# GpSimd makes half of a quantised product, and ScalarE weighs half of the last chunk's experts by token

## The chip, the cores and the metric

The kernel runs on one core of a Trainium2 chip. The core's engines each work through an instruction stream of their own and wait for each other by semaphores: TensorE (PE), VectorE (DVE), ScalarE (ACT), GpSimd (POOL), and SyncE (SP), which issues DMAs. The metric is the device time of one execution in microseconds, median of several.

## What is computed

Two layers, each a chain of four parts on 2,048 tokens of 128 features. The change touches two of them. The third part of layer 0 is a gated network with fake quantisation: activations to 16 bits with one scale for the whole tensor, so each scale needs the maximum over everything.

```python
def act_qdq(x):
    qmax = 2.0 ** (ACT_BITS - 1) - 1.0
    scale = jnp.maximum(jnp.max(jnp.abs(x)) / qmax, 1e-12)
    return jnp.clip(jnp.round(x / scale), -qmax - 1.0, qmax) * scale
...
x = act_qdq(x)
up = act_qdq(x @ lpbq_dequant(w_up).T)
gate = act_qdq(x @ lpbq_dequant(w_gate).T)
sig = fixed_qdq_u16(jax.nn.sigmoid(gate))
gate = act_qdq(gate * sig)
o = act_qdq(gate * up)
return o @ lpbq_dequant(w_down).T
```

The last part of layer 1 is attention whose projections are mixtures of 16 experts, with the router's weights `w` (token x expert):

```python
q, k, v = moe_proj(q_proj), moe_proj(k_proj), moe_proj(v_proj)
attn = jax.nn.softmax(q @ k.T / sqrt(h))   # within a batch
o = attn @ v
z = jnp.einsum('ne,nh->enh', w, o)
out = jnp.einsum('enh,ehc->nc', z, o_proj)
```

and the result is added to the layer's input.

## The kernel before

Everything lies in SBUF, features on the 128 partitions and tokens along the row, in four chunks of 512 (`cc(c)`); a tile of 128 tokens is `bb_(b)`. All five engines' streams are written out by hand (`tensor`, `scalar`, `vector`, `gpsimd`, `sync`); `q.wait_ge(name, n)` lets an engine wait for the n-th signal of a name. The table `LANES` puts many names on few semaphores and counts each name's signals.

**The quantised network (place A).** The 384 hidden features are three tensors of 128x2048, `UP[j]` and `GT[j]`. Both are turned into whole numbers: ScalarE writes `up` as int16 into `U16Q` (L1008, 3 of 2,048 columns) and `gate*sig` as int16 into `G16` (L1012); the first half of the first tensor is converted by VectorE (L1544). In a loop over four pieces of 1,024, 1,024, 2,048 and 2,048 columns (`pieces`) VectorE multiplies (L1548) and takes the largest absolute value (L1550, written by the helper on L1456), signalling `o_max`. The four maxima are joined (L1459), TensorE turns the column into a row (`quant_turn`, L588), VectorE takes the maximum of the row (L1463) and makes the scale (L1470 to L1475), and ScalarE converts the product with it (L1016), VectorE splits the result into two f16 numbers (L1561, L1563) and TensorE multiplies (L625). Ahead of the last `quant_turn` TensorE does eight products whose result nobody reads, behind it six more; the eight wait for a maximum:

```python
q.wait_ge("o_max", 3)
for _ in range(8):
    e.matmul(BK[6][:, :], FW16[:, 0, 0, :], FW16[:, 0, 0:4, :], start=True, stop=True)
quant_turn(4)
```

GpSimd has no work there: between L1867 of `i` = 3 and L1865 of `i` = 4 (splitting the projections' weights into f16 halves, P16) it waits for `o_lo` 12.

**The output of the experts (place B).** For chunks 0 to 2 TensorE multiplies a tile of attention output with four experts at a time (`output(n)`, L803, three f16 products of 512 columns into the banks 3, 6 and 7 in turn), and VectorE adds the four 128x128 blocks, each weighed by the token's weight, to `XT` (`gather(n)`, L1741). The list `groups` names chunk, tile and four experts of each n; 44 to 47 are the last tile of chunk 2. The last chunk goes another way: VectorE multiplies the attention output (features x tokens, bank 4) with each expert's weights laid out along the tokens (L1807, 16 products of 128x512, `zw`), and TensorE multiplies each with the expert's matrix in f32, adding all 16 up in a bank for each tile (`weighed_output`, L835, `tile`). VectorE adds each tile to `XT` with the softmax's factor (L1815, `done`), and SyncE sends it out (L1983).

## Time and profile before

| | |
|---|---|
| median of 3 runs | 490.58 us (490.44 to 490.92) |
| the profiled execution | 490.49 us, of which its span is 488.7 us |
| PE busy | 438.8 us (90%) |
| DVE busy | 410.8 us (84%) |
| ACT busy | 244.6 us (50%) |
| POOL busy | 62.7 us (13%) |
| chain that ended last | PE 25%, DVE 25%, issue 4%, ACT 1% (the rest below the groups shown) |

The profile shows one execution. A line of a timeline has the start, the time (of all of a merged group), engine, source line, operation, output and inputs, shapes, how many, and in brackets how long the engine was idle before it and who ended that. Where a helper writes an instruction, the line is the helper's. An f32 product of TensorE is two records. The granted clock (PEclk) is a share of TensorE's full speed. Idle time of an engine that isn't the bound costs nothing.

### The profile page before, as it was taken

Reading aid. Unit: us, or ns where it says so; the run is one execution under the profiler, and the core shown is the slowest. Engines: PE = TensorE matmul, PEld = TensorE weight load, DVE = VectorE, ACT = ScalarE, POOL = GpSimd, SP = SyncE. Lnnn points to the kernel's source line nnn. Section 1 sums busy time; section 2 is a strip of 40 time slices with the busy share of each in tenths; the row PEclk is TensorE's granted clock in tenths of the full one; section 3 lists DMA queues with packets and bytes.
Section 4 is the critical chain, followed back from the end, with each engine's and each line's share of the span. In section 5 each row is a group of like instructions: output and inputs, shape, how many; then the busy total and the mean of one; then the engine's idle time right before and its main releaser. Section 6 shows DMA issues by size and latency. Waiting matters only on the chain.

```text
span 488.7 us, 9719 instructions
## 1 busy us (share of the span) xinstructions
PE 438.8 (90%) x3791; PEld 304.3 (62%) x3791; DVE 410.8 (84%) x919; ACT 244.6 (50%) x446; POOL 62.7 (13%) x77
## 2 busy tenths in 40 slices
PE   8999999998899989401899899999999999999997
PEld 6447999987358754100279876667656666655676
DVE  6997889777797659999876689986998999989786
ACT  5976555473856629895655554336224222423110
POOL 0007000000590705500081000000000000000000
PEclk9999999999999999855999998999999999999999
DMA  8979997950560003403330016545863000000000
GB/s 271 352 303 392 386 382 301 372 240 23 150 173 1 1 0 129 130 0 129 130 98 1 1 43 221 170 178 180 280 237 97 7 12 7 5 7 7 6 7 28
DMA packets 24629, 66.71 MB, mean 137 GB/s; under 512 B 3108, under 2 KB 6567, under 8 KB 24455
## 3 DMA queue, kind: packets, MB, share of 16 engines
q1 hardware_dynamic: 24144, 65.98, 37.7%
q8 instruction: 30, 0.49, 0.4%
q10 hardware_dynamic: 438, 0.11, 0.1%
q14 instruction: 17, 0.13, 0.1%
HBM read 38.68 MB, written 1.18 MB: 82 GB/s over the span
## 4 chain that ended last, share of the span: by engine, by line
PE 25%; DVE 25%; issue 4%; ACT 1%; DVEq 0%
PE bk L758 8%; DVE XT L1741 6%; DVE X L1729 4%; PE bk L766 4%; DVE RA L1769 4%; PE bk L803 3%; PE bk L625 2%; DVE RA L1548 1%; DVE WK L1590 1%; PE bk L778 1%; PE bk L634 1%; PE bk L668 1%; PE bk L685 1%; DVE QS L1456 1%; PE bk L694 1%
## 5 line engine op out<-in xcount | busy, mean ns | idle before, releaser
L758 PE MATMUL bk<-X,RB 128*128 128x512 f16 x384 | 94.6, 383 | 0.6 <-DVE X L1729 0.4
L1061 ACT ACTIVATE X<-RA 128x512 f16<-128x512 f32 x64 | 40.3, 630 | 100.9 <-DVE RA L1769 84.7
L1741 DVE SCALAR_TENSOR_TENSOR XT<-bk,WK,XT 128x128 f32<-128x128 f32 x192 | 67.0, 349 | 5.4 <-issue 0.2
L758 PEld LDWEIGHTS bk<-X,RB 128*128 128x128 f16 x384 | 37.0, 98 | 42.3 <-DVE X L1729 1.6
L766 PEld LDWEIGHTS bk<-RB,X 128*128 128x128 f16 x768 | 48.4, 98 | 15.4 <-issue 0.6
L766 PE MATMUL bk<-RB,X 128*128 128x128 f16 x768 | 53.5, 220 | 0.0
L1729 DVE TENSOR_TENSOR X<-RA,X 128x512 f16<-128x512 f32 x64 | 43.9, 685 | 1.1 <-ACT X L1061 1.1
L899 ACT ACTIVATE WK<-bk 128x512 f32<-128x512 f32 x48 | 28.6, 595 | 27.5 <-PE bk L414 21.9
L803 PE MATMUL bk<-RB,RA 128*128 128x512 f16 x144 | 38.8, 379 | 0.9 <-DVE RA L1786 0.9
L1357 DVE SCALAR_TENSOR_TENSOR RB<-WK,WCOL,bk 128x512 f32<-128x512 f32 x32 | 23.7, 744 | 10.0 <-ACT WK L899 10.0
L414 PE MATMUL bk<-X,RC 128*128 128x128 f16 x480 | 29.7, 219 | 0.0
L1363 DVE TENSOR_TENSOR RB<-RB 128x512 f16<-128x512 f32 x36 | 25.7, 715 | 3.9 <-ACT RB L909 3.6
L414 PEld LDWEIGHTS bk<-X,RC 128*128 128x128 f16 x480 | 27.9, 98 | 0.9
L909 ACT ACTIVATE RB<-RB 128x512 f16<-128x512 f32 x36 | 22.4, 623 | 5.2 <-DVE RB L1357 5.0
L409 PE MATMUL bk<-X,STG 128*128 128x512 f16 x96 | 22.9, 379 | 0.5 <-DVE X L1171 0.4
L1456 DVE TENSOR_REDUCE QS<-RA 128x1 f32<-128x512 f32 (+2 forms) x28 | 22.4, 836 | 0.1
L588 PE MATMUL bk<-PK1T,QS 128*128 128x128 f32 x5 | 1.9, 384 | 20.5 <-DVE QS L1459 20.5
L1848 POOL TENSOR_SCALAR RA<-RA,ROPE 128x128 f32<-128x128 f32 x16 | 9.4, 586 | 81.4 <-ACT RA L929 81.4
L409 PEld LDWEIGHTS bk<-X,STG 128*128 128x128 f16 x96 | 9.2, 97 | 16.1 <-issue 5.2
L443 PE MATMUL bk<-RB,RC 128*128 128x128 f16 x240 | 16.6, 219 | 2.0 <-DVE RB L1363 2.0
L803 PEld LDWEIGHTS bk<-RB,RA 128*128 128x128 f16 x144 | 12.6, 98 | 7.3 <-DVE RA L1786 1.3
L1867 POOL TENSOR_TENSOR RB<-X,RB 128x1024 f16<-128x1024 f32 x8 | 17.1, 2132 | 0.7
(345 smaller groups left out, 887.3 us busy)
## 6 DMA issues: line engine op xcount, KB each, us to landing
RC<-RA SPq DMA_DIRECT2D x20, 768.0 KB, 5.2
STG<-RA SPq DMA_DIRECT2D x8, 768.0 KB, 5.3
RC<-expert_weights SPq DMA_DIRECT2D x22, 256.0 KB, 6.2
RC<-in_wx SPq DMA_DIRECT2D x7, 768.0 KB, 8.2
X<-in_w SPq DMA_DIRECT2D x8, 512.0 KB, 3.5
RA<-RA SPq DMA_DIRECT2D x4, 768.0 KB, 5.0
STG<-expert_weights SPq DMA_DIRECT2D x12, 256.0 KB, 6.5
QT<-expert_weights SPq DMA_DIRECT2D x8, 256.0 KB, 4.6
```

Of the source, the lines that this page charges most:

```text
L409: t = e.matmul(bank[:, :], W16[:, o:o + 128], X16[:, xp, cc(a)], start=(n == 0), stop=(n == 2))
L414: t = e.matmul(bank[:, bb_(jj)], w[:, o:o + 128], X16[:, xp, bb_(a)], start=(n == 0), stop=(n == 2))
L758: t = e.matmul(BK[m][:, :], P16[:, wp, wo:wo + 128], ZH[:, n % 4, xp, :], start=(e1 == 0 and i == 0), stop=(e1 == 15 and i == 2))
L766: t = e.matmul(BK[2][:, bb_(b)], ZH[:, n % 4, xp, bb_(b)], P16[:, wp, wo:wo + 128], start=(e1 == 0 and b == 0 and i == 0), stop=(e1 == 15 ...
L803: t = e.matmul(bank_o(n)[:, :], OT16[:, xp, bb_(4 * c + b)], P16[:, wp, 6144 + 512 * g:6656 + 512 * g], start=(i == 0), stop=(i == 2))
L899: e.activation(ge[u % 3], pair(k)[0][:, :], ACT.Gelu_apprx_tanh, scale=1.0 / WS).then_inc(S("gelu"), 1)
L1061: e.activation(ZH[:, r, 0, :], zf[r], ACT.Copy).then_inc(S("z_hi"), 1)
L1357: stt(hf[u % 3], ge[u % 3], w, pair(k)[1][:, :], ALU.mult, ALU.mult).then_inc(S("gated"), 1)
L1363: tt(H16[:, u % 3, 1, :], hf[u % 3], H16[:, u % 3, 0, :], ALU.subtract).then_inc(S("h_lo"), 1)
L1456: return red(dst, src, X_AX, ALU.max, apply_absolute_value=True)
L1729: tt(ZH[:, n % 4, 1, :], zf[n % 4], ZH[:, n % 4, 0, :], ALU.subtract).then_inc(S("zlo"), 1)
L1741: stt(XT[:, bb_(t_)], bank_o(n)[:, bb_(i)], RW[:, t_, e1:e1 + 1], XT[:, bb_(t_)], ALU.mult, ALU.add).then_inc(S("acc"), 1)
```

## The change

**A.** The tensors are cut into six halves of 1,024 columns; halves 1, 3 and 5 go to GpSimd (`BY_POOL`), 0, 2 and 4 to VectorE (`BY_VECTOR`). For VectorE's halves ScalarE writes `up` as int32 into two PSUM banks (two instructions of 512), so a product is two instructions. For GpSimd's halves ScalarE rounds in place: it adds a large number (MAGIC) as bias, and GpSimd takes it off again. Of `gate` ScalarE takes it off itself for halves 1 and 5, GpSimd for half 3. All maxima stay on VectorE. `quant_turn(4)`'s eight products wait for the fifth of six maxima. SyncE's weight loads of experts 8 to 11 wait for `o_max` 6 where they waited for `ot_ff` 4.

**B.** Of the last chunk, VectorE and TensorE do experts 0 to 7 the old way (`PRE` = 8). Experts 8 to 15 are done like the earlier chunks' by `output(n)`, n = 48 to 55, for which VectorE splits the attention output into f16 halves (`last_halves`). ScalarE copies the blocks of n = 44 to 55 out of the bank, weighed by token (`late`), and VectorE sums them over the experts and adds the sum to `XT` (`sum_up`, five times). `late(44)` stands between ScalarE's `softmax(3)` and `ptt(3)`.

```diff
+        halves = [(i // 2, slice(1024 * (i % 2), 1024 * (i % 2) + 1024)) for i in range(6)]
+        BY_POOL, BY_VECTOR = (1, 3, 5), (0, 2, 4)
+        U16P = {i: [BK[i + n][:, :].bitcast(I32) for n in range(2)] for i in BY_VECTOR}
...
+        PRE, LATE = 8, 44
+        groups += [(3, b, g) for b in range(4) for g in range(PRE // 4, 4)]
+        GRP = (16 - PRE) // 4
...
         def tensor(e):
-            q.wait_ge("o_max", 3)
+            q.wait_ge("o_max", 5)
             for _ in range(8):
...
             def output(n):
                 c, b, g = groups[n]
                 q.wait_ge("ot_lo", c + 1)
-                q.wait_ge(*(("acc", 4 * (n - 2)) if n >= 3 else ("wts", 3)))
+                q.wait_ge(*(("late_w", n - 2 - LATE) if n - 3 >= LATE else ("acc", 4 * (n - 2)) if n >= 3 else ("wts", 3)))
...
-            for e1 in range(12):
-                for b in range(4):
-                    weighed_output(e1, b)
-                if e1 in (0, 4):
-                    output(46 + (e1 == 4))
-            for b in range(4):
-                for e1 in range(12, 16):
+            n = 46
+            for e1 in range(PRE):
+                for b in range(4):
                     t = weighed_output(e1, b)
-                t.then_inc(S("tile"), 1)
+                    if e1 == PRE - 1:
+                        t.then_inc(S("tile"), 1)
+                for _ in range(1 if e1 < 3 else 2):
+                    if n < len(groups):
+                        output(n)
+                        n += 1
...
         def scalar(e):
-            for j in range(3):
+            q.wait_ge("magic", 2)
+            for i in range(6):
+                j, h = halves[i]
                 q.wait_ge("quant", Q_STEPS[2])
-                e.activation(U16Q[j], UP[j], ACT.Identity, scale=rq(2)).then_inc(S("up16"), 1)
-            for i, (j, h) in enumerate(pieces):
-                if i:
-                    q.wait_ge("quant", Q_STEPS[3])
+                if i in BY_POOL:
+                    t = e.activation(UP[j][:, h], UP[j][:, h], ACT.Identity, bias=MAGC, scale=rq(2))
+                else:
+                    for n in range(2):
+                        t = e.activation(U16P[i][n], UP[j][:, cc(n)], ACT.Identity, scale=rq(2))
+                t.then_inc(S("up16"), 1)
+            for n, (i, off) in enumerate(((1, 0), (1, 1), (2, 0), (3, 0), (4, 0), (5, 0), (5, 1))):
+                j, h = halves[i]
+                q.wait_ge("quant", Q_STEPS[3])
+                if off:
+                    q.wait_ge("gated16", n)
+                    e.activation(GT[j][:, h], GT[j][:, h], ACT.Identity, bias=MAGN).then_inc(S("gated16"), 1)
+                elif i in BY_POOL:
+                    e.activation(GT[j][:, h], GT[j][:, h], ACT.Identity, bias=MAGC, scale=rq(3)).then_inc(S("gated16"), 1)
+                else:
                     e.activation(G16[j][:, h], GT[j][:, h], ACT.Identity, scale=rq(3)).then_inc(S("gated16"), 1)
...
+            def late(n):
+                c, b, g = groups[n]
+                t_ = 4 * c + b
+                q.wait_ge("late", n - LATE + 1)
+                q.wait_ge("rw", c + 1)
...
+                for i in range(4):
+                    e1 = 4 * g + i
+                    t = e.activation(WGT[n - LATE][:, bb_(i)], bank_o(n)[:, bb_(i)], ACT.Copy, scale=RW[:, t_, e1:e1 + 1])
+                t.then_inc(S("late_w"), 1)
+
             softmax(3)
+            late(44)
             ptt(3)
+            for n in range(45, len(groups)):
+                late(n)
 
         def vector(e):
...
+            GATED = {0: ("gated16_0", 1), 2: ("gated16", 3), 4: ("gated16", 5)}
+
+            def ot_product(i):
+                j = halves[i][0]
+                q.wait_ge(*GATED[i])
+                q.wait_ge("up16", i + 1)
+                for n in range(2):
+                    t = tt(GT[j][:, cc(n)], G16[j][:, cc(n)], U16P[i][n], ALU.mult)
+                t.then_inc(S("ot_ff"), 1)
...
-            for e1 in range(16):
+            q.wait_ge("rs", 4)
+            tt(RW[:, 12:16, :], RW[:, 12:16, :], RS[:, 12:16].unsqueeze(2).to_broadcast([128, 4, 16]), ALU.mult).then_inc(S("rw"), 1)
+
+            def sum_up(i):
+
+                t_, first, many = (11, 0, 4) if i == 0 else (11 + i, 4 + GRP * (i - 1), GRP)
+                q.wait_ge("late_w", first + many)
+                q.wait_ge("otmm", 4)
+                src = XF[:, 0:2048] if i == 0 else RA[:, 512 * (first - 4):512 * (first - 4 + many)]
+                red(SUM[:, i, :], src.rearrange("p (e n) -> p n e", n=128), X_AX, ALU.add).then_inc(S("sum"), 1)
+                q.wait_ge("sum", i + 1)
+                q.wait_ge("turned", 4)
+                tt(XT[:, bb_(t_)], XT[:, bb_(t_)], SUM[:, i, :], ALU.add).then_inc(S("summed"), 1)
...
+            for e1 in range(PRE):
                 q.wait_ge("otmm", 4)
                 q.wait_ge("zlo", NI)
                 q.wait_ge("qkvmm", 12)
                 tt(ZW[e1], BK[4][:, :], WR[16 + e1], ALU.mult).then_inc(S("zw"), 1)
-                if e1 in (1, 4, 7, 10):
-                    gather({1: 44, 4: 45, 7: 46, 10: 47}[e1])
+                if e1 == 1:
+                    last_halves()
+            sum_up(0)
             for b in range(4):
                 t_ = 12 + b
+                sum_up(b + 1)
                 q.wait_ge("tile", b + 1)
                 q.wait_ge("rs", 4)
-                q.wait_ge("turned", 4)
+                q.wait_ge("summed", b + 2)
                 stt(XT[:, bb_(t_)], BK_T[b][:, 0:128], RS[:, t_:t_ + 1], XT[:, bb_(t_)], ALU.mult, ALU.add).then_inc(S("done"), 1)
 
         def gpsimd(e):
...
+                if i == 4:
+                    for m, n in enumerate(BY_POOL):
+                        j, h = halves[n]
+                        q.wait_ge("up16", n + 1)
+                        q.wait_ge("gated_ff", 5)
+                        e.tensor_scalar(UP[j][:, h], UP[j][:, h], MAGIC, None, ALU.subtract).then_inc(S("pool_whole"), 1)
+                    for m, n in enumerate(BY_POOL):
+                        j, h = halves[n]
+                        q.wait_ge("gated16", (2, 4, 7)[m])
+                        if n == 3:
+                            e.tensor_scalar(GT[j][:, h], GT[j][:, h], MAGIC, None, ALU.subtract).then_inc(S("pool_whole"), 1)
+                        q.wait_ge("pool_whole", (1, 4, 4)[m])
+                        e.tensor_tensor(GT[j][:, h], UP[j][:, h], GT[j][:, h], ALU.mult).then_inc(S("ot_pool"), 1)
```

How the order on the engines moves. VectorE at place A, with the bank numbers; before, from the conversion of the first half (L1544) to the joining of the maxima:

```order
L1544 TENSOR_SCALAR WK<-RA,RQ 128x1024
L1548 TENSOR_TENSOR RA<-WK,RC 128x1024
L1456 TENSOR_REDUCE QS<-RA 128x1
L1548 TENSOR_TENSOR RA<-WK,RC 128x1024
L1456 TENSOR_REDUCE QS<-RA 128x1
L1548 TENSOR_TENSOR RA<-WK,RC 128x2048
L1456 TENSOR_REDUCE QS<-RA 128x1
L1548 TENSOR_TENSOR RA<-WK,RC 128x2048
L1456 TENSOR_REDUCE QS<-RA 128x1
L1459 TENSOR_REDUCE QS<-QS 128x1
```

The same stretch of VectorE now:

```order
L1608 TENSOR_SCALAR WK<-RA,RQ 128x1024
L1599 TENSOR_TENSOR RA<-WK,bk0 128x512
L1599 TENSOR_TENSOR RA<-WK,bk1 128x512
L1505 TENSOR_REDUCE QS<-RA 128x1
L1599 TENSOR_TENSOR RA<-WK,bk2 128x512
L1599 TENSOR_TENSOR RA<-WK,bk3 128x512
L1505 TENSOR_REDUCE QS<-RA 128x1 x2
L1599 TENSOR_TENSOR RA<-WK,bk4 128x512
L1599 TENSOR_TENSOR RA<-WK,bk5 128x512
L1505 TENSOR_REDUCE QS<-RA 128x1 x3
L1508 TENSOR_REDUCE QS<-QS 128x1
```

Half of the products have gone, all maxima (now six, in the order of halves 0, 2, 1, 4, 3, 5) have stayed, and the second product now stands behind ScalarE's third `gated16`. ScalarE at the same place, `up` and then `gate` (MG are the two columns of the large number); before:

```order
L1008 ACTIVATE RC<-RA,RQ 128x2048 x3
L1012 ACTIVATE WK<-RA,RQ 128x1024
L1012 ACTIVATE WK<-RA,RQ 128x2048 x2
L1016 ACTIVATE WK<-RA,RQ 128x512 x12
```

And now:

```order
L1032 ACTIVATE bk<-RA,RQ 128x512 x2
L1029 ACTIVATE RA<-RA,MG,RQ 128x1024
L1032 ACTIVATE bk<-RA,RQ 128x512 x2
L1029 ACTIVATE RA<-RA,MG,RQ 128x1024
L1032 ACTIVATE bk<-RA,RQ 128x512 x2
L1029 ACTIVATE RA<-RA,MG,RQ 128x1024
L1041 ACTIVATE RA<-RA,MG,RQ 128x1024
L1039 ACTIVATE RA<-RA,MG 128x1024
L1043 ACTIVATE WK<-RA,RQ 128x1024
L1041 ACTIVATE RA<-RA,MG,RQ 128x1024
L1043 ACTIVATE WK<-RA,RQ 128x1024
L1041 ACTIVATE RA<-RA,MG,RQ 128x1024
```

Three instructions for `up` have become nine, and the first `gate` half that VectorE needs (the first L1043) is the third of its kind. TensorE at place B, the end of its stream (L803 is `output`, L835 `weighed_output`); before, to its last instructions but a few:

```order
L835 MATMUL bk<-WEFF,RA 128x128 x4
L803 MATMUL bk<-RB,RA 128x512 x3
L835 MATMUL bk<-WEFF,RA 128x128 x12
L835 MATMUL bk<-WEFF,QT 128x128 x4
L803 MATMUL bk<-RB,RA 128x512 x3
L835 MATMUL bk<-WEFF,QT 128x128 x12
L835 MATMUL bk<-WEFF,STG 128x128 x18
```

TensorE now, to its end (L817 and L849 are the same two, ahead of this piece stand two groups of each):

```order
L817 MATMUL bk<-RB,RA 128x512 x3
L849 MATMUL bk<-WEFF,RA 128x128 x4
L817 MATMUL bk<-RB,RA 128x512 x3
L849 MATMUL bk<-WEFF,RA 128x128 x4
L817 MATMUL bk<-RB,RA 128x512 x6
L849 MATMUL bk<-WEFF,QT 128x128 x4
L817 MATMUL bk<-RB,RA 128x512 x6
L849 MATMUL bk<-WEFF,QT 128x128 x4
L817 MATMUL bk<-RB,RA 128x512 x6
L849 MATMUL bk<-WEFF,QT 128x128 x4
L817 MATMUL bk<-RB,RA 128x512 x3
L849 MATMUL bk<-WEFF,QT 128x128 x4
```

All ten groups `output(46)` to `output(55)` now stand ahead of the last four f32 products, which are the ones that signal `tile`. VectorE at place B, its last rows before (L1807 weighing, L1741 `gather`, L1815 the last accumulation):

```order
L1807 TENSOR_TENSOR QT<-bk,RC 128x512 x3
L1741 SCALAR_TENSOR_TENSOR XT<-bk,WK,XT 128x128 x4
L1807 TENSOR_TENSOR STG<-bk,RC 128x512 x3
L1741 SCALAR_TENSOR_TENSOR XT<-bk,WK,XT 128x128 x4
L1807 TENSOR_TENSOR STG<-bk,RC 128x512 x3
L1807 TENSOR_TENSOR PK0T<-bk,RC 128x512 x2
L1815 SCALAR_TENSOR_TENSOR XT<-bk,SM,XT 128x128 x4
```

And now, from the last three weighings (L1879 sums over the experts, L1882 adds the sum, L1903 is the last accumulation); two further such threes follow:

```order
L1893 TENSOR_TENSOR QT<-bk,RC 128x512 x3
L1879 TENSOR_REDUCE RA<-X 128x128
L1882 TENSOR_TENSOR XT<-XT,RA 128x128
L1879 TENSOR_REDUCE RA<-RA 128x128
L1882 TENSOR_TENSOR XT<-XT,RA 128x128
L1903 SCALAR_TENSOR_TENSOR XT<-bk,SM,XT 128x128
L1879 TENSOR_REDUCE RA<-RA 128x128
L1882 TENSOR_TENSOR XT<-XT,RA 128x128
L1903 SCALAR_TENSOR_TENSOR XT<-bk,SM,XT 128x128
```

The four accumulations no longer stand in a row: a sum and an addition stand ahead of each.

## Rows read from the trace of the kernel before

**Rows 1.** Timeline of VectorE at place A: start us, us, engine, line, operation.
```profile
220.88 1.23 DVE L1548 TENSOR_TENSOR RA<-WK,RC 128x1024 f32<-128x1024 int16 x1
222.14 1.22 DVE L1456 TENSOR_REDUCE QS<-RA 128x1 f32<-128x1024 f32 x1
223.28 1.22 DVE L1548 TENSOR_TENSOR RA<-WK,RC 128x1024 f32<-128x1024 int16 x1
...
232.50 2.29 DVE L1456 TENSOR_REDUCE QS<-RA 128x1 f32<-128x2048 f32 x1
```

**Rows 2.** Timeline of ScalarE at place A; then its groups by form there.
```profile
215.84 5.77 ACT L1008 ACTIVATE RC<-RA,RQ 128x2048 int16<-128x2048 f32 x3
...
236.41 7.46 ACT L1016 ACTIVATE WK<-RA,RQ 128x512 int16<-128x512 f32 x12 [9.98 <-DVE RQ L1475]
...
L1012 ACT ACTIVATE WK<-RA,RQ 128x1024 int16<-128x1024 f32 x1 | 1.1, 1132 | 0.0
```

**Rows 3.** Timeline of TensorE at place A; then a window (0.81 is PEclk).
```profile
230.32 3.60 PE L612 MATMUL bk<-FW 128*128 128x512 f16 x8 [11.41 <-DVE QS L1456]
235.03 0.32 PE L588 MATMUL bk<-PK1T,QS 128*128 128x128 f32 x1 [1.11 <-DVE QS L1459]
...
234.00:235.00 1.00, 0.00 (x0) 0.00 (x0) 0.94 (x2) 0.00 (x0) 0.00 (x0) 0.81 0.82 304
```

**Rows 4.** Timeline of GpSimd: one pass of each kind.
```profile
38.64 2.35 POOL L1825 TENSOR_TENSOR RB<-RB 128x1024 f32<-128x1024 f32 x1
...
190.11 2.13 POOL L1867 TENSOR_TENSOR RB<-X,RB 128x1024 f16<-128x1024 f32 x1
...
245.31 1.04 POOL L1865 TENSOR_SCALAR RB<-X 128x1024 f16<-128x1024 f32 x1 [42.75 <-DVE RA L1563]
246.43 2.14 POOL L1867 TENSOR_TENSOR RB<-X,RB 128x1024 f16<-128x1024 f32 x1
```

**Rows 5.** Timeline of VectorE at place B.
```profile
467.71 0.69 DVE L1807 TENSOR_TENSOR RA<-bk,PK0T 128x512 f32<-128x512 f32 x1 [0.68 <-PE bk L790]
...
481.75 1.28 DVE L1807 TENSOR_TENSOR PK0T<-bk,RC 128x512 f32<-128x512 f32 x2
483.62 0.35 DVE L1815 SCALAR_TENSOR_TENSOR XT<-bk,SM,XT 128x128 f32<-128x128 f32 x1 [0.58 <-PE bk L835]
...
486.30 0.35 DVE L1815 SCALAR_TENSOR_TENSOR XT<-bk,SM,XT 128x128 f32<-128x128 f32 x1 [0.54 <-PE bk L835]
```

**Rows 6.** Timeline of ScalarE: four 128x128 with a bias column, and place B.
```profile
285.03 1.14 ACT L1044 ACTIVATE RA<-bk,BSEL 128x128 f32<-128x128 f32 x4
...
465.23 0.21 ACT L1090 ACTIVATION_READ_ACCUMULATOR WK<-bk,SM 128x1 f32 x1
465.87 0.60 ACT L1095 ACTIVATE RA<-bk 128x512 f32<-128x512 f32 x1 [0.42 <-PE bk L784]
```

**Rows 7.** Timeline of TensorE at place B.
```profile
468.46 1.16 PE L835 MATMUL bk<-WEFF,RA 128*128 128x128 f32 x8 [0.79 <-DVE RA L1807]
469.45 0.81 PE L803 MATMUL bk<-RB,RA 128*128 128x512 f16 x3
470.10 3.02 PE L835 MATMUL bk<-WEFF,RA 128*128 128x128 f32 x24
472.96 1.06 PE L835 MATMUL bk<-WEFF,QT 128*128 128x128 f32 x8
473.85 0.81 PE L803 MATMUL bk<-RB,RA 128*128 128x512 f16 x3
```

**Rows 8.** Place B as a window: busy us of PE, PEld, DVE, ACT, POOL.
```profile
467.70:486.70 19.00, 17.17 (x134) 15.55 (x134) 16.30 (x36) 0.00 (x0) 0.00 (x0) 1.00 0.05 16
```

**Rows 9.** Groups of VectorE by form: two-operand products, strided and not; 128x128.
```profile
L1444 DVE TENSOR_TENSOR RA<-RA,bk 128x512 f32<-128x512 f32 x8 | 8.1, 1063 | 2.1 <-PE bk L567 2.1
...
L1583 DVE TENSOR_TENSOR XT<-XT,bk 128x512 f32<-128x512 f32 x4 | 2.7, 681 | 0.1
...
L1694 DVE TENSOR_TENSOR WK<-WK,SM 128x128 f32<-128x128 f32 x1 | 0.3, 291 | 0.0
```

More of the change, by code:

```diff
@@ L169, in program @@
         RQ = sb("RQ", [128, 10])
+        MG = sb("MG", [128, 2])
+        MAGC, MAGN = MG[:, 0:1], MG[:, 1:2]
         def pk0(n):
@@ L1818, in gpsimd @@
             q = Eng(e, by_home)
+            e.memset(MAGC, MAGIC).then_inc(S("magic"), 1)
+            e.memset(MAGN, -MAGIC).then_inc(S("magic"), 1)
             q.wait_ge("expert_lo", 16)
@@ L1981, in sync @@
                     t_ = 4 * c + b
-                    q.wait_ge(*(("acc", 4 * groups.index((c, b, 3)) + 4) if c < 3 else ("done", b + 1)))
+                    q.wait_ge(*(("done", b + 1) if c == 3 else ("summed", 1) if t_ == 11 else ("acc", 4 * groups.index((c, b, 3)) + 4)))
                     e.dma_start(out[bb_(t_), :], XT[:, bb_(t_)]).then_inc(S(f"out{c}"), 16)
```

58 lines of the change are left out of this document (39 added, 19 removed).

## The prediction

> **What bounds the kernel now.** I read the page first (engines and slices), then the timelines of the two places that the change touches, engine by engine, and last the groups by form for the price of one operation. Both places lie on the path that sets the end, one after the other, so their gains and losses add.
>
> Place A is the last quantisation, of the product `gate*up` (219.97 to 236.41 us). VectorE multiplies and takes maxima back to back from 220.88 to 234.79 [rows 1]; ScalarE has delivered its last input by 226.4 and is then idle for 9.98 us until the new scale comes [rows 2]. So VectorE is the bound there. TensorE does next to nothing, but it carries the maximum across partitions (a transpose at 235.03), and ahead of that it runs eight idle-work products of 512 columns at 230.32 to wake its clock [rows 3]. They took 3.60 us, about 0.43 each from start to start (512 columns at the lower level, 1.2 GHz), and were over 1.1 us before the transpose was wanted. Keep this slack in mind.
>
> Place B is the end. VectorE starts weighing the attention output at 467.71 and raises its last `done` at 486.65 [rows 5]; it is busy 16.30 of 19.00 us there, TensorE 17.17 [rows 8]. The two are nearly level: relieving one shows the other.
>
> The profiled execution took 490.49 us (span 488.7), the median is 490.58. I sum against 490.49.
>
> **Part A: the quantised network.** VectorE loses three of the six halves' products. What it must still do: convert half 0, three products (two instructions of 512 each, one operand now in PSUM, 1.28 us a pair as the 512-wide pairs of [rows 5] show), six maxima (1.22 us, 1.14 from start to start where nothing is waited for [rows 1]).
>
> But product 2 now waits for ScalarE's third `gated16`. ScalarE starts as before at 215.84 and issues for `up` three halves of 1,024 (1.04 us a step: 1.132 less some 0.09 of overlap, by the 1,024-wide first of L1012) and six pieces of 512 into PSUM (0.62 a step, L1016) [rows 2]. PSUM as a target isn't in these rows; I take the price of SBUF, since the same engine reads PSUM at about the same cost. That is 3.12 + 3.70 = 6.8 us, to 222.65, against 5.8 before. Then come (1, scaled), (1, magic taken off, which waits for the first to drain), (2): 1.13 + 1.04 + 1.13, so the third is out at 226.0. VectorE has been done with half 0 at 223.4: it idles 2.6 us, and of the 3.4 us that three removed products (1.14 to 1.22 each) were to give less than one is left. From there: product 2 at 226.0, maximum 2 at 227.3, maximum 1 at 228.45, product 4 at 229.6, maximum 4 at 230.9, maximum 3 at 232.05 to 233.25, maximum 5 at 233.2 to 234.4. On VectorE alone that gains 0.4 us against 234.79.
>
> GpSimd: one-input pass 1.04, two-input f32 pass of 1,024 2.35 [rows 4]. Product 1 starts when its two inputs are there at 224.95, is out at 227.3 (maximum 1 at 228.45 waits for nothing); product 3 after its own subtraction at 230.8 (maximum 3 at 232.05, covered); product 5 at 233.2, level with maximum 5. So GpSimd is covered, the last half barely; a late half 5 costs nothing until it is 2.2 us late, for the reason that follows.
>
> TensorE is what is late next. The eight idle-work products wait for `o_max` 3 before, 5 now. Before, the third maximum ended at 230.27 and a 2,048-wide product and maximum (4.5 us) still followed. Now the fifth maximum ends at 233.25 and only 1.2 us follow, while eight products at the low clock need 8 x 0.43 = 3.4 us. They are queued ahead of the transpose, so it starts at 233.3 + 3.4 = 236.7 instead of 235.03: +1.7; it would be ready for at 234.6 otherwise. The granted clock was 0.81 over 234 to 235 [rows 3], so it rose inside that microsecond, some four after the eight began; counted from 233.3 that is 237.2, so the transpose itself now falls into the low level and its 0.32 us may take up to twice as long: +0.1 to +0.3, I take 0.1. **A costs +1.8 us.** Bounds: if ScalarE's instructions with both a bias and a scale column cost 0.09 more each, +2.2; if `gated16` came so early that VectorE never idled, the fifth maximum would end at 230.7, the transpose start at 234.1, and A gain 0.9. GpSimd's later weights (P16), and the weight DMAs of experts 8 to 11 (now behind `o_max` 6, two microseconds later on SP's queue, with the last two `w2` loads behind them) are needed tens of microseconds later: nothing.
>
> **Part B: the end.** ScalarE gets `late(44)` between the softmax and `ptt(3)`. The softmax ends at 465.44; four 128x128 copies take 1.14 us (L1044's four), so `ptt(3)` starts at 466.45 and not 465.87 [rows 6]: +0.6 for the attention output and for VectorE's first weighing, 467.71 to 468.3.
>
> VectorE then does 8 weighings (0.60 a step), the f16 halves of the output (0.69 and 0.69), and five sums. TensorE's queue is the one that counts: from 469.05 (468.46 + 0.6) it does eight groups of four f32 products and ten groups `output(46..55)` in between. A group of four took 0.89 (472.96 to 473.85), a group `output` 0.65 (469.45 to 470.10) [rows 7]. The first `tile` comes in the eighth group, behind all outputs: 7 x 0.89 + 10 x 0.65 = 12.7, and 0.4 for its own product: 482.2. VectorE has had nothing left since about 479 to 481. Before, `tile` 1 was met at 483.62 [rows 5]. So 8 x 4 fewer f32 products (7.1 us) were exchanged for eight more f16 groups (5.2), less the 0.6 of the later start: 1.4 us earlier, not more. ScalarE's copies (1.14 a group, each output waits for the group three before) stay 0.8 us or more ahead of TensorE: free.
>
> After `tile` 1, though, the work left is larger. Before, one 0.35 us accumulation for each of four tiles, TensorE-paced: 483.62 to 486.65, 3.0 us. Now, on VectorE alone and in this order: accumulate 0; then three times a sum over 1,024 values, an addition of 128x128 (0.29), an accumulation (0.35), each waiting for the one before. The sum reads with a stride of 128 floats. That is the unknown price. From below: the contiguous maximum over 1,024, 1.22. From above: L1444, the one VectorE operation here whose SBUF operands are strided (16 floats), takes 1.063 for 512 elements where L1583, the same operation with contiguous operands, takes 0.681 [rows 9]. Off both goes a fixed 0.15 (1.22 at 1,024 and 2.29 at 2,048 leave that), so 1.79 ns an element against 1.05: 1,024 elements 1.98. L1444 is nearest, since it is the only strided row; I take 1.98. The step is then 1.98 + 0.29 + 0.35, three hand-overs of 0.03, less 0.08 of overlap: 2.6 us; the end is 482.2 + 3 x 2.6 + 0.35 = 490.35, against 486.65: **B costs +3.7 us.** With 1.22 the step is 1.84 and the end 488.1: +1.4. The strided sum over 2,048 (3.8) and the first over 1,024 end at 481, under `tile` 1.
>
> The Trainium skill has a rule for this (Advanced Engine Details and Errata, "Memory Cachelines"): SBUF is read in lines of 16 bytes, and an access pattern that moves to another line with every element pays a penalty. By that rule the sum is dear, which agrees with L1444; without it B would be the +1.4. It names no factor; mine is L1444's.
>
> Sum: 490.49 + 1.8 + 3.7 = **496.0 us**. Between the places the work is the same and is only later.
>
> **Rivals.** (1) *The strided sums cost as contiguous ones.* For it: L1444 also writes with a stride, the sums write contiguously, so its excess may be the write's. 490.5 + 1.8 + 1.4 = 493.7. (2) *The relief of VectorE counts in full, faster than before.* At A the maxima are not held by `gated16`, at B `tile` 1 isn't late: with contiguous sums VectorE's chain then ends B 3.5 us earlier than in (1), 2.1 before 486.65, and A gives 0.9: 487.5. It decides where ScalarE's third `gated16` comes by 223.4 and TensorE's first `tile` by 478.6. Against it: ScalarE's rows put the one at 226.0, TensorE's the other at 482.2, and neither row leaves three microseconds. (3) *GpSimd is the bound of A.* If its f32 passes are slowed beside VectorE, or slower in place, maximum 5 comes late. At 1.3 times their price (three two-input passes and a subtraction in a row from 224.95) it ends at 236.7, still level with the eight products; at 1.5 times at 238.3, and A is +3.5: 490.5 + 3.5 + 3.7 = 497.7. Its two-input pass at 246.43, beside a busy VectorE, took 2.14 us, and the one at 190.11 took 2.13 [rows 4], which speaks against it. (4) *The eight products don't hold the transpose* (they run faster than in [rows 3]): A is then -0.4 to +0.3, with the sums as forecast 494.0. The engine has been idle for 14 us, so nothing speaks for it.
>
> **How the numbers follow.** Forecast 0.52, its own range 495.2 to 496.9; (1) 0.31; (2) 0.04; (3) 0.04; (4) 0.04; within 0.2% by pieces of both signs 0.05. The range 493.2 to 497.2 takes in forecast, (1) and (4) with the bounds of A, and leaves out some 0.13. 0.2% is 1.0 us, about what a measurement of this kernel tells from none. Faster by more than that 0.04, same 0.05, slower 0.91.
>
> **What would show it.** In the changed profile: VectorE idle for some 2.6 us before product 2, released by ScalarE; eight products of 512 from about 233.3 with the transpose directly behind them at 236.7, and no VectorE work under them in the last two microseconds; the scale out for ScalarE's `o16` at 238.2 instead of 236.41. At the end (all 1.8 later): VectorE idle before its first accumulation, released by TensorE; three steps of 2.6 us behind it, sums of 2.0 us. I am wrong if the transpose follows maximum 5 at once, if the sums take 1.2, or if `tile` 1 comes before the second sum is done.

## The result and the profile after

The changed kernel took 498.73 us (median of 5, 498.48 to 499.73) against 490.58 (median of 5, 490.38 to 490.92): 1.0169 times, 95% interval 1.0154 to 1.0183. It is 8.15 us slower where 5.5 was forecast, above the range. The profiled execution took 498.77 us, its span 496.6.

**Place A** ends 4.1 us later, not 1.8. VectorE's timeline of the kernel after, from the conversion of half 0 to the maximum of the turned row (columns as in [rows 1], which it answers):

```profile
220.05 1.59 DVE L1608 TENSOR_SCALAR WK<-RA,RQ 128x1024 int16<-128x1024 f32 x1
221.67 1.28 DVE L1599 TENSOR_TENSOR RA<-WK,bk 128x512 f32<-128x512 int16 x2
...
226.33 1.28 DVE L1599 TENSOR_TENSOR RA<-WK,bk 128x512 f32<-128x512 int16 x2 [2.11 <-ACT WK L1043]
...
229.35 1.22 DVE L1505 TENSOR_REDUCE QS<-RA 128x1 f32<-128x1024 f32 x1 [0.49 <-POOL RA L1963]
...
234.52 1.22 DVE L1505 TENSOR_REDUCE QS<-RA 128x1 f32<-128x1024 f32 x1 [1.50 <-POOL RA L1963]
236.82 1.22 DVE L1505 TENSOR_REDUCE QS<-RA 128x1 f32<-128x1024 f32 x1 [1.09 <-POOL RA L1963]
...
239.47 0.29 DVE L1512 TENSOR_REDUCE QS<-bk 128x1 f32<-128x128 f32 x1 [1.23 <-PE bk L602]
```

The first gap is the forecast one: product 2 waits for ScalarE until 226.33 (forecast 226.0). The three after it, 0.49, 1.50 and 1.09 us, are released by GpSimd's products (L1963), and none of them was forecast. (The first gap is 2.11 us and not 2.6 because the conversion of half 0 took 1.59 us for 0.74.) GpSimd's own timeline there (kernel after; its kinds of pass answer [rows 4]):

```profile
218.32 8.68 POOL L1956 TENSOR_SCALAR RA<-RA 128x1024 f32<-128x1024 f32 x3 [15.90 <-ACT RA L1029]
226.97 2.35 POOL L1963 TENSOR_TENSOR RA<-RA 128x1024 f32<-128x1024 f32 x1
229.29 2.76 POOL L1961 TENSOR_SCALAR RA<-RA 128x1024 f32<-128x1024 f32 x1
232.14 4.65 POOL L1963 TENSOR_TENSOR RA<-RA 128x1024 f32<-128x1024 f32 x2
```

GpSimd never idles from 218.32 to 236.8. The products cost what [rows 4] say, 2.35. The subtractions (L1956, L1961) took 2.9 and 2.76 us each and not 1.04. TensorE's timeline (kernel after; it answers [rows 3]):

```profile
235.79 3.53 PE L626 MATMUL bk<-FW 128*128 128x512 f16 x8 [16.93 <-DVE QS L1505]
239.16 0.27 PE L602 MATMUL bk<-PK1T,QS 128*128 128x128 f32 x1
```

The eight products start when the fifth maximum ends (235.74), and the transpose follows directly behind them, 4.1 us later than at 235.03 in [rows 3].

**Place B** is as forecast. VectorE's timeline (kernel after; it answers [rows 5]):

```profile
478.67 3.68 DVE L1879 TENSOR_REDUCE RA<-X 128x128 f32<-128x2048 f32 x1
...
486.54 0.35 DVE L1903 SCALAR_TENSOR_TENSOR XT<-bk,SM,XT 128x128 f32<-128x128 f32 x1 [1.69 <-PE bk L849]
486.80 1.87 DVE L1879 TENSOR_REDUCE RA<-RA 128x128 f32<-128x1024 f32 x1
488.71 0.29 DVE L1882 TENSOR_TENSOR XT<-XT,RA 128x128 f32<-128x128 f32 x1
489.11 0.35 DVE L1903 SCALAR_TENSOR_TENSOR XT<-bk,SM,XT 128x128 f32<-128x128 f32 x1
...
494.22 0.35 DVE L1903 SCALAR_TENSOR_TENSOR XT<-bk,SM,XT 128x128 f32<-128x128 f32 x1
```

VectorE waits 1.69 us for the first tile, then come three steps of 2.56 us, each a sum (1.87), an addition and an accumulation. ScalarE's timeline shows the late start (kernel after; it answers [rows 6]):

```profile
469.66 1.16 ACT L1169 ACTIVATE X<-bk,WK 128x128 f32<-128x128 f32 x4
470.66 0.64 ACT L1126 ACTIVATE RA<-bk 128x512 f32<-128x512 f32 x1
```

Three stretches between landmarks of VectorE let the kernels be compared without the drift of the rest. *A* runs from the start of the maximum of the third turned row (218.95 in the kernel before) to that of the fourth (235.39); *middle* from there to the copy of the last chunk's first result (460.80); *B* from there to the end of the last accumulation (486.65). Each number is worked out from the two landmarks of one trace:

| kernel | A | middle | B |
|---|---|---|---|
| before | 16.44 | 225.41 | 25.85 |
| after | 20.57 | 225.66 | 29.44 |
| a_only | 20.75 | 225.74 | 25.84 |
| b_only | 16.60 | 225.82 | 29.43 |
| two_ops | 18.58 | 225.37 | 29.44 |
| two_warm | 16.58 | 226.03 | 29.44 |
| a_mend | 16.57 | 225.80 | 25.83 |
| near | 20.75 | 225.38 | 27.52 |
| b_best | 16.60 | 226.15 | 23.87 |
| b_best2 | 16.44 | 225.45 | 23.88 |
| best | 16.57 | 225.99 | 23.88 |
| best2 | 16.58 | 225.79 | 23.86 |

After against before: +4.13, +0.25 and +3.59, together 7.97; ahead of A it gains 0.05, and between the last accumulation and the execution's own time lie 4.20 us where there were 3.84. That makes the 8.28 between the two profiled executions.

The last of these terms, 0.36, was in no sum. It lies outside the profiled span: every execution of the kernels with both parts (after, two_ops, two_warm, near, best, best2) took 2.09 to 2.22 us more than its span, every one of the kernels with one part or none 1.74 to 1.85. No run shows what it is.

### The profile page after: what moved, and what is told of

It reads as the page before. It is cut to its first block, busy times and chain, and to the rows that moved or that the text cites. A ratio compares the mean times of both kernels' runs of the same rounds, so it can differ in the third digit from the quotient of the medians.

```text
span 496.6 us, 9706 instructions
## 1 busy us (share of the span) xinstructions
PE 435.9 (88%) x3751; PEld 300.8 (61%) x3751; DVE 412.8 (83%) x912; ACT 262.0 (53%) x504; POOL 81.3 (16%) x86
## 4 chain that ended last, share of the span: by engine, by line
PE 53%; DVE 29%; ACT 6%; issue 5%; POOL 3%; DMA 2%; SPq 1%; DVEq 0%; ACTq 0%; POOLq 0%
PE bk L772 9%; PE bk L428 5%; PE bk L780 5%; DVE XT L1808 5%; PE bk L817 4%; DVE QS L1505 3%; DVE X L1796 3%; PE bk L457 3%; PE bk L423 3%; DVE RA L1836 2%; DMA STG<-RA 2%; PE bk L639 2%; PE bk L551 2%; POOL RA L1956 1%; PE bk L560 1%
## 5 line engine op out<-in xcount | busy, mean ns | idle before, releaser
L1808 DVE SCALAR_TENSOR_TENSOR XT<-bk,WK,XT 128x128 f32<-128x128 f32 x176 | 61.4, 349 | 4.9
L817 PE MATMUL bk<-RB,RA 128*128 128x512 f16 x168 | 44.8, 379 | 0.9 <-DVE RA L1853 0.9
L1505 DVE TENSOR_REDUCE QS<-RA 128x1 f32<-128x512 f32 (+1 forms) x30 | 22.7, 791 | 3.2 <-POOL RA L1963 3.1
L817 PEld LDWEIGHTS bk<-RB,RA 128*128 128x128 f16 x168 | 15.0, 98 | 9.0 <-DVE RA L1853 1.3
L626 PE MATMUL bk<-FW 128*128 128x512 f16 x8 | 3.5, 620 | 16.9 <-DVE QS L1505 16.9
```

The source lines that it names most:

```text
L817: t = e.matmul(bank_o(n)[:, :], OT16[:, xp, bb_(4 * c + b)], P16[:, wp, 6144 + 512 * g:6656 + 512 * g], start=(i == 0), stop=(i == 2))
L1505: return red(dst, src, X_AX, ALU.max, apply_absolute_value=True)
L1808: stt(XT[:, bb_(t_)], bank_o(n)[:, bb_(i)], RW[:, t_, e1:e1 + 1], XT[:, bb_(t_)], ALU.mult, ALU.add).then_inc(S("acc"), 1)
```

## The experiments

**Each part alone.** a_only has the end as before, b_only the quantised network as before. Of their edits, first two pieces of a_only's:

```diff
-        PRE, LATE = 8, 44
...
-            late(44)
```

and two of b_only's:

```diff
-            q.wait_ge("o_max", 5)
+            q.wait_ge("o_max", 3)
...
-                q.wait_ge(*(("ffs", 3) if b < 4 else ("o_max", 6)))
+                q.wait_ge(*(("ffs", 3) if b < 4 else ("ot_ff", 4)))
```

> Place A alone, place B as in the kernel before. Theory (the two losses are separate and add): the changed profile has the scale of the last quantisation out at 240.45 us where it was 236.38, so +4.1 us and 494.7 us. Rival (A's lateness is partly taken up later, or starts something else): anything else than +4.1; the stretch between the places was 0.25 us longer in the changed trace, which with A alone would show as 494.9.

> Place B alone, place A as in the kernel before. Theory: +3.6 us, 494.2 us, with steps of 2.57 us behind the first tile. Rival (B depends on what A did to the phase of the engines): B alone is more than 0.7 us off 3.6.

Measured: a_only 494.86 us, ratio 1.0085 (1.0069 to 1.0102); b_only 494.51, 1.0107 (1.0061 to 1.0154); the kernel before on the same chip 490.8. So +4.1 and +3.7, together 7.8 of the 8.15 (by the medians; b_only's ratio is raised by one of its four executions, 498.73 beside three at 494.4 to 494.6). Each part costs its own place what it costs in the whole change (A 20.75, B 29.43 in the table). Within the span the parts add; the rest of the 8.15 is the 0.36 outside the span, which neither part has alone.

**The form of GpSimd's subtraction.** two_ops is the kernel after with the same sum written as two operations:

```diff
-                        e.tensor_scalar(UP[j][:, h], UP[j][:, h], MAGIC, None, ALU.subtract).then_inc(S("pool_whole"), 1)
+                        e.tensor_scalar(UP[j][:, h], UP[j][:, h], -MAGIC, 1.0, ALU.add, ALU.mult).then_inc(S("pool_whole"), 1)
...
```

(and the same on L1961.)

> The changed kernel; GpSimd takes the large number off with two operations in one pass (add -MAGIC, times 1.0) instead of one. Theory 1 (the form with one operation is what is slow on GpSimd, since the pass of the kernel before that took 1.04 us had two): passes fall from 2.76 to about 1.05 us, product 5 is out at 233.2 instead of 236.8, A costs what was predicted (+1.8 to 2.0) and the kernel takes 496.5 us. Theory 2 (f32 output or being in place is what is slow, since that pass wrote f16 elsewhere): the passes stay at 2.76 us and the kernel at 498.7.

Measured: 496.22 us (496.04 to 496.55), ratio 1.0114 (1.0097 to 1.0131), +5.4 to 490.8 on its chip, where the prediction had 5.5. GpSimd's timeline of two_ops:

```profile
218.14 1.04 POOL L1956 TENSOR_SCALAR RA<-RA 128x1024 f32<-128x1024 f32 x1 [15.46 <-ACT RA L1029]
...
228.60 4.66 POOL L1963 TENSOR_TENSOR RA<-RA 128x1024 f32<-128x1024 f32 x2
```

and VectorE's:

```profile
219.87 0.74 DVE L1608 TENSOR_SCALAR WK<-RA,RQ 128x1024 int16<-128x1024 f32 x1
...
234.56 0.16 DVE L1508 TENSOR_REDUCE QS<-QS 128x1 f32<-128x6 f32 x1
```

The pass is 1.04, GpSimd is through at 233.26, the maxima are joined at 234.56 (forecast 234.4, plus the join), and VectorE's conversion of half 0 is back at 0.74 from 1.59. TensorE's timeline of two_ops has what is left:

```profile
233.44 3.60 PE L626 MATMUL bk<-FW 128*128 128x512 f16 x8 [14.77 <-DVE QS L1505]
236.83 0.42 PE L602 MATMUL bk<-PK1T,QS 128*128 128x128 f32 x1
```

The forecast had 233.3 and 236.7. The form of the subtraction was worth 2.0 us of A's 4.1. What is left, 18.58 against 16.44, is 2.1 where 1.8 was forecast and 2.2 was the bound for dearer instructions on ScalarE.

**The eight products.** two_warm is two_ops with the eight products waiting for the third maximum again:

```diff
-            q.wait_ge("o_max", 5)
+            q.wait_ge("o_max", 3)
```

> The changed kernel with GpSimd's subtraction in two operations, and TensorE's eight idle-work products waiting for the third maximum instead of the fifth. In the run with the two operations alone the joined maximum was ready at 234.72 us and the transpose started at 236.83, behind the eight products. Theory (the eight products hold the transpose): it starts at 234.8, the kernel is 2.0 to 2.1 us faster than that run, 494.1 us, and A as a whole is then level with the kernel before (the maximum is joined at 234.56 against 234.82). Rival (the transpose was late for another reason, or the clock falls again in the longer gap and gives the time back): less than 1 us of it returns.

Measured: 494.8 us (493.8 to 495.66, ten runs), ratio 1.0078 (1.0056 to 1.0099); the kernel before on this chip 490.35. A is 16.58: the other 2.0 us, and the transpose starts at 234.72 as expected, so nothing but 0.14 is left of A's loss in its own stretch. The time, though, missed the expectation (494.1): the distance to the kernel before fell by 1.0 us, from 5.4 to 4.45, and the two profiled executions lie 1.4 apart. The middle gives 0.66 of the 2.0 back (226.03 for 225.37). TensorE's next 36 products ran with the full clock in two_ops and took 8.12 us; in two_warm the granted clock was still 0.50 over 238 to 239, where they had begun at 237.82, and they took 8.51. The rival, that the clock gives some of the time back, is therefore right in part. The kernel stands 0.7 above b_only, and half of that is the 0.36 outside the span.

a_mend has both repairs and the end of before.

> Nothing is left out. Part A alone, with GpSimd's subtraction written as two operations (add the negative number, times 1.0) and TensorE's eight products waiting for the third maximum; the end is that of the kernel before. If the two causes found so far are all that A costs, the scale is out for ScalarE's conversion at 236.2 (236.41 before) and the time is that of before within 0.2% (490 to 491.3). If the clock lost in the gap behind the transpose counts, the 36 products after it start 0.4 us longer and the time is 491.2 to 491.8. If A were a gain once mended it would be under 489.4; its trace has no place for that, since VectorE still idles for ScalarE's third gate half.

Measured: 490.63 us against 490.61, ratio 1.0008 (0.999 to 1.0026). Part A, repaired, alone, costs nothing that can be measured and gives nothing. The relief that was taken off VectorE is spent in the wait for ScalarE. VectorE's timeline of a_mend:

```profile
226.67 1.28 DVE L1571 TENSOR_TENSOR RA<-WK,bk 128x512 f32<-128x512 int16 x2 [2.96 <-ACT WK L1033]
...
235.09 0.16 DVE L1480 TENSOR_REDUCE QS<-QS 128x1 f32<-128x6 f32 x1
```

The gap of 2.96 us eats most of the 3.4 us that the three removed products gave. The rest goes into maxima of 1,024 for maxima of 2,048 and products in two instructions: the maxima are joined 15.85 us behind the start of A, in the kernel before 15.87. The alternative in the expectation, a loss to TensorE's clock (491.2 to 491.8), isn't borne out by the median; what the traces show of the clock is told under the hardware below.

**The stride of the sums.** near is the kernel after with ScalarE writing the weighed blocks so that a token's experts lie side by side, and VectorE summing them contiguously (this is VectorE's line; ScalarE's target changes with it):

```diff
-                red(SUM[:, i, :], src.rearrange("p (e n) -> p n e", n=128), X_AX, ALU.add).then_inc(S("sum"), 1)
+                red(SUM[:, i, :], src.rearrange("p (n e) -> p n e", n=128), X_AX, ALU.add).then_inc(S("sum"), 1)
```

> The changed kernel; ScalarE writes each weighed value beside those of the other experts (its writes are strided by 8 or 16 floats), so that VectorE's sums over the experts read contiguous memory. Theory (reading with a stride is what makes a sum of 1,024 values 1.87 us instead of 1.22): the three sums behind the first tile take 1.22, the kernel is 1.95 us faster, 496.8 us. Rival 1 (128 outputs of one instruction cost the excess, not the stride of the reads): sums stay at 1.87, 498.7. Rival 2 (the strided writes slow ScalarE as much): its groups of four copies go from 1.14 to 1.5 us or more, TensorE waits for the banks and the first tile is later.

Measured: 496.7 us, ratio 1.0105 (1.0054 to 1.0156); B is 27.52 for 29.44. VectorE's timeline of near:

```profile
478.56 2.28 DVE L1885 TENSOR_REDUCE RA<-X 128x128 f32<-128x2048 f32 x1
...
486.43 0.35 DVE L1909 SCALAR_TENSOR_TENSOR XT<-bk,SM,XT 128x128 f32<-128x128 f32 x1 [3.81 <-PE bk L849]
486.70 1.21 DVE L1885 TENSOR_REDUCE RA<-RA 128x128 f32<-128x1024 f32 x1
...
488.34 0.35 DVE L1909 SCALAR_TENSOR_TENSOR XT<-bk,SM,XT 128x128 f32<-128x128 f32 x1
```

The kernel is 2.0 us faster than the change, as expected (1.95). The sum falls from 1.87 to 1.21 and the step from 2.56 to 1.91. The first tile comes when it came before (486.43), and VectorE only waits longer for it, 3.81 us: TensorE sets that moment, as forecast. ScalarE pays with 1.26 us for four blocks where it took 1.14 to 1.20, under cover.

**The order of the end.** b_best keeps A as before; its end has near's layout, all five sums ahead of the four accumulations, and two outputs earlier in TensorE's stream:

```diff
-            sum_up(0)
+            for b in range(5):
+                sum_up(b)
             for b in range(4):
-                sum_up(b + 1)
                 q.wait_ge("tile", b + 1)
...
+            output(46)
...
+            output(47)
...
-                for _ in range(1 if e1 < 3 else 2):
+                for _ in range((0, 1, 1, 2, 2, 2, 0, 0)[e1]):
```

> Place A as in the kernel before. Place B as changed, with three edits: contiguous sums as in the run named near; all five sums ahead of the four last accumulations; output(46) ahead of the last attention product and output(47) behind it, where TensorE was idle 0.55 and 0.78 us, so that the first tile is 1.3 us earlier. Theory (B loses because the first tile is late and strided sums stand behind it): B turns from +3.6 to -2 to -2.6 us, 488.0 to 488.6 us. Rival (VectorE's whole work at B, not its order, is the bound): -0.5 or less.

> Nothing is left out. A second look at the kernel with A as before and B with contiguous sums ahead of the accumulations and two outputs earlier (first: 489.8, ratio 0.9925 to 0.9989, where its trace had place B 2.0 us shorter and the rest 0.9 us later). If the 0.9 us was the variation of the run, the time is 488.4 to 489.3. If it belongs to the kernel, 489.6 to 490.1.

Measured: 489.8 us on the first chip (ratio 0.9957, 0.9925 to 0.9989) and 488.95 on the second, beside 490.61 for the kernel before (0.9973, 0.9949 to 0.9997). On the first chip the medians lie only 0.55 us apart; the ratio there is helped by three of the 25 executions of the kernel before, at 494.6 to 495.2. The first missed its expectation of 488.0 to 488.6; it is 0.9 us above the second, and the table shows where the two traces differ: 0.16 in A and 0.70 in the middle, both outside the change. B is 23.87 and 23.88, 2.0 us under the kernel before, as expected. Not all of it reaches the time: the four tiles now leave together, and from the last accumulation to the end of the span it takes 2.7 us where it took 2.05, so some 1.3 remain. VectorE's timeline of b_best2:

```profile
468.47 0.69 DVE L1862 TENSOR_TENSOR RA<-bk,PK0T 128x512 f32<-128x512 f32 x1 [1.46 <-PE bk L796]
...
474.58 2.27 DVE L1848 TENSOR_REDUCE RA<-X 128x128 f32<-128x2048 f32 x1
...
481.81 1.22 DVE L1848 TENSOR_REDUCE RA<-RA 128x128 f32<-128x1024 f32 x1 [0.26 <-ACT RA L1156]
483.07 0.29 DVE L1851 TENSOR_TENSOR XT<-XT,RA 128x128 f32<-128x128 f32 x1
483.28 1.12 DVE L1872 SCALAR_TENSOR_TENSOR XT<-bk,SM,XT 128x128 f32<-128x128 f32 x4
```

At the end stand four accumulations in a row, 1.12 us, where the change had 8.0 us of sums and accumulations behind its first tile (486.54 to 494.57). Once it has begun to weigh (468.47), VectorE waits only 0.26 us, for ScalarE's last copies, and no longer for TensorE's tiles. So with this order the shift of work from VectorE and TensorE to ScalarE pays. Of the 5.6 us between 29.44 and 23.88, near's layout is 1.9; the order of the sums and the two earlier outputs were changed together, and no run parts their 3.65.

best is b_best's end with the repaired A; best2 is the same kernel on the second chip.

> The run named b_best with place A as in two_warm. Theory: A adds 0 to -0.3 us to it, 487.8 to 488.6 us. Rival (A's parts don't add with B's): more than 0.7 us off b_best.

> Nothing is left out. The same end as b_best2 with A mended as in a_mend. If A mended is level, the same time as b_best2 within 0.4 us, and the difference of a_mend to before is repeated here; if A mended costs 0.8 us, 0.8 above b_best2.

Measured: 489.77 us, ratio 0.9984 (0.9956 to 1.0013), and 489.52, 0.9981 (0.9957 to 1.0004), against 489.8 and 488.95 for b_best on the same two chips. Neither expectation was met: best was to take 487.8 to 488.6, and best2 lies 0.57 above b_best2, between the two cases of its expectation. In A, middle and B the kernels with the repaired A don't differ from the others by more than two traces of b_best do (table), and what they have more is the 0.36 outside the span that comes with both parts. b_best is the one version here whose interval lies below 1 on both chips. The gain is small, 0.55 and 1.7 us by the medians.

**Which of GpSimd's forms are dear.** pool_forms and pool_forms2 are the kernel before with extra passes of 128x1024 on a spare buffer (SCA and SCB) while GpSimd has no work. Of pool_forms2 four of the six passes (each waits for the one before):

```diff
+                        e.tensor_scalar(SCA, SCA, 1.0, None, ALU.mult).then_inc(ff.next(), 1)
...
+                        e.tensor_scalar(SCA, SCA, 1.0, None, ALU.add).then_inc(ff.next(), 1)
...
+                        e.tensor_scalar(SCA, SCA, 1.0, 1.0, ALU.mult, ALU.mult).then_inc(ff.next(), 1)
...
+                        e.tensor_scalar(SCA, SCB, 1.0, 1.0, ALU.mult, ALU.mult).then_inc(ff.next(), 1)
```

> The kernel before, with twelve extra passes of 128x1024 on GpSimd between 204 and 245 us, each behind the last, on memory that nobody reads: f32 subtraction in place with one operation, two multiplications in place, the same to another place, add and multiply in place, subtraction to f16, f32 product of two; all twice. Theory 1 (one operation is slow): first and fifth 2.76 us, the others of one input 1.05. Theory 2 (f32 output is slow): first to fourth 2.76, fifth 1.05. Theory 3 (in place is slow): first, second and fourth 2.76. A row that repeats later beside VectorE's two-input products (from 221 us) longer than earlier would show that the engines hold each other up.

> Nothing is left out; this is the kernel before with extra GpSimd passes on a spare 128x1024 f32 buffer, twice each: one-operation multiplication in place; one-operation addition in place; mult and mult in place; mult and mult to another place, in the direction opposite to the first look; add and mult to another place; mult and mult to f16 in another place. If what makes a pass slow is having only one operation, the first two take 2.8 us and the others 1.05. If it is also writing f32 to another place, the fourth and fifth take 2.9 too and the last 1.04 (the kernel's own pass to f16). If only subtraction is slow, all but the fourth and fifth take 1.05.

Each ran once (496.13 and 501.64 us; the passes delay VectorE, so these times mean nothing else). GpSimd's timeline of pool_forms2, the second turn: L1870 and L1872 have one operation (a multiplication, an addition), L1874 to L1880 have two, L1880 writes f16:

```profile
225.48 2.77 POOL L1870 TENSOR_SCALAR RB<-RB 128x1024 f32<-128x1024 f32 x1
228.33 2.77 POOL L1872 TENSOR_SCALAR RB<-RB 128x1024 f32<-128x1024 f32 x1
231.19 1.23 POOL L1874 TENSOR_SCALAR RB<-RB 128x1024 f32<-128x1024 f32 x1
232.50 1.05 POOL L1876 TENSOR_SCALAR RB<-RB 128x1024 f32<-128x1024 f32 x1
233.63 1.05 POOL L1878 TENSOR_SCALAR RB<-RB 128x1024 f32<-128x1024 f32 x1
234.76 2.96 POOL L1880 TENSOR_SCALAR RB<-RB 128x1024 f16<-128x1024 f32 x1
```

One operation takes 2.77, be it a multiplication or an addition, and in pool_forms a subtraction, to f32 (2.78) or f16 (2.77). Two operations take 1.05, to another place (L1876, L1878) as in place (1.04 in pool_forms; the 1.23 here began under a product of VectorE's that ended 0.3 us later). The expectation that a target at another place is dear, formed on a pass of 2.96 us in pool_forms, fell: L1876 and L1878 write f32 elsewhere in 1.05. What makes 2.96 is VectorE, whose timeline of pool_forms2 has beside L1880:

```profile
233.75 3.06 DVE L1549 TENSOR_TENSOR RA<-WK,RC 128x2048 f32<-128x2048 int16 x1
```

It ends at 236.81, and L1880 at 237.72, 0.91 us later, nearly the 1.05 of a whole pass: GpSimd stood almost still under it. The 2.96 in pool_forms ends the same way, at 233.22, 0.91 us behind a product of VectorE's.

## Why the prediction was wrong, step by step

**The step that failed** is the term of A "GpSimd: one-input pass 1.04". It was taken from L1865 in [rows 4], a pass of two operations (times 1.0, times 1.0), and put on L1956 and L1961, which have one. Such a pass costs 2.77 here, 2.7 times as much. The four of them took 11.4 us where 4.2 were reckoned, so GpSimd's chain, which was to wait for ScalarE until 224.95, became one that never waits. With 1.05 in its place two_ops gave the forecast to 0.2 us in the rows and in the total (496.22). That the total fits so well is in part luck: A was 2.1 for 1.8, B 3.6 for 3.7, and the 0.36 outside the span was in no sum. A hint stood in the trace of before and was not read. GpSimd's timeline there, a single-operation pass and a two-operand addition on the same 16 columns:

```profile
41.73 0.32 POOL L1833 TENSOR_SCALAR ROPE<-PK1T,COL 128x16 f32<-128x16 f32 x1
...
43.24 0.22 POOL L1837 TENSOR_TENSOR ROPE<-ROPE 128x16 f32<-128x16 f32 x1
```

At 1,024 columns the pass with two operands is the dearer by [rows 4]; at 16 it is the cheaper. That was a hint that the one-operation form isn't L1865's, not a proof: L1833's factor is a column in memory and L1956's is a number in the instruction.

**Rival (3)** was the near one (497.7). It was given 0.04 since two-input passes beside a busy VectorE were not slowed ([rows 4]), and they were not: 2.35. The evidence spoke of the passes that were priced rightly and said nothing of the others. It was also weaker than it seemed: what VectorE ran beside the pass at 246.43 has one operand in PSUM (L1567), and pool_forms2 shows that beside a product with both in SBUF a GpSimd pass takes 2.96 for 1.05. Being in place, the doubt that rival (3) named, costs nothing (1.04). The range ended at 497.2 because the one-input price had no upper bound of its own; "its f32 passes slower in place" named the doubt and left it unpriced.

**The eight products** held the transpose as forecast: they start at the end of the fifth maximum and take 3.37 us to the transpose (3.4). In the change itself that moment is set by GpSimd, 235.74 for 233.3. two_ops and two_warm give each of the two causes 2.0 us of A. The 0.1 for a slower transpose fits two_ops (0.42 for 0.32); in the change it took 0.27, at a granted clock of 0.94 over 239 to 240. Rival (4) is out: the eight took 3.53 to 3.60 in every kernel.

**ScalarE's delay** held: third `gated16` at 226.3 (forecast 226.0). ScalarE's timeline of the kernel after has a pass with bias and scale, and the third with a scale alone:

```profile
222.85 1.23 ACT L1041 ACTIVATE RA<-RA,MG,RQ 128x1024 f32<-128x1024 f32 x1
...
225.16 1.13 ACT L1043 ACTIVATE WK<-RA,RQ 128x1024 int16<-128x1024 f32 x1
```

The first costs 0.10 more, the 0.09 of the bound, and with the form of the subtraction mended A came out at 2.1, near that bound's 2.2.

**What VectorE pays for its neighbour** wasn't in the sum: its conversion of half 0 took 1.59 for 0.74 beside the slow subtraction, 0.85 us that went into the gap before product 2 (2.11 us; 2.96 in two_ops).

**Part B** held in each term: `ptt(3)` at 470.66, which is 0.46 later (forecast 0.6) once the 4.33 us are off by which the place starts late (465.13 for 460.80); the first tile at 486.54, that is 482.2 and the 4.33; sums of 1.87 for 1.98; three steps of 2.56 for 2.6; +3.6 for +3.7. Rival (1), contiguous price, is out: near shows 1.21 when the stride is gone, with nothing else in the step changed. The read of L1444 was the right row to go by. By the Trainium skill (Advanced Engine Details and Errata, "Memory Cachelines") reads that take a new 16-byte line with every element are slower; this trace agrees, with 1.87 against 1.21 for 1,024 and 3.68 against 2.28 for 2,048.

**Rival (2)**, the relief in full, did not come about in either place, for the reasons given. At B b_best2 shows what it took: all sums under TensorE's work, so that the relief isn't spent behind the last tile.

## What to carry to other kernels

These are lessons of this one kernel. Price an operation by a row of the same form: engine, number of operations, target and stride, not just engine and size; where the row is of another form, that gap is an unknown cost with two bounds. Work moved to an idle engine must be priced together with what its slowest pass does to the order of everything that waits behind it, and warm-up work that waits for a count of signals must be looked at again when the signals' order changes. Work that was taken off the bounding engine pays only if what remains of it stands ahead of the last wait, not behind it.
